# A chunked state-space scan on one core: the triangular solve taken for two units together, and three operand loads moved in the queue

## The reference, cut to what matters

```python
def step(s, inp):
    q_, w_, k_, v_, a_, b_ = inp
    sa = jnp.einsum('bhij,bhj->bhi', s, a_)
    s = s * w_[:, :, None, :] + sa[..., None] * b_[:, :, None, :] + v_[..., None] * k_[:, :, None, :]
    return (s, jnp.einsum('bhij,bhj->bhi', s, q_))
_, y = jax.lax.scan(step, s0, (qt, wt, kt, vt, at, bt))
```

## Time and profile before

| | |
|---|---|
| median of 3 runs | 6624.89 us (6621.29 to 6627.57) |
| the profiled execution | 6620.48 us |
| its span, first to last instruction | 6618.7 us |
| the scan | about 1435 to 2910 us of it |
| busy in 1700 to 2700 us | PE 879, weight loads 862, DVE 892, POOL 729, ACT 489 us |
| DMA engines there | busy 0.60, 131 GB/s, nearly all on SP's queue |
| granted TensorE clock there | 1.00 (2.4 GHz) |
| solve steps (L1167, L1171) | 960 + 960, 330.2 + 326.6 us on DVE |
| b and k expansions (L954) | 1024, 419.3 us on POOL |

### The profile page before, as it was taken

How to read it: one execution, slowest core, us unless ns; L and a number is a source line. 1 busy time by engine, 2 the same in 40 slices (tenths; PEclk the granted TensorE clock), 3 DMA queues, 4 the chain that set the end, 5 groups by cost and what they waited for, 6 DMA issues and landing times. The chain is left out here.

```text
span 6618.7 us, 201409 instructions
## 1 busy us (share of the span) xinstructions
PE 5523.2 (83%) x70816; PEld 4552.2 (69%) x70816; DVE 4142.5 (63%) x13289; ACT 3445.6 (52%) x10441; POOL 2667.4 (40%) x3872
## 2 busy tenths in 40 slices
PE   5555556648888888866599999999979999999999
PEld 4555555548888888854477777777757777777777
DVE  4666666658888989944355555555535555555555
ACT  3555555534444444434355555555535555555555
POOL 1333332236777777720133333333324343333433
PEclk7777777779999999986799999999989999999999
DMA  2222223335565566545200000000010000000000
GB/s 60 62 62 58 61 62 64 64 84 131 129 133 129 130 133 131 130 104 182 93 15 12 14 12 15 12 14 12 15 40 16 19 17 17 20 17 19 17 17 17
DMA packets 999524, 387.22 MB, mean 59 GB/s; under 512 B 775664, under 2 KB 948720, under 8 KB 998512
## 3 DMA queue, kind: packets, MB, share of 16 engines
q1 hardware_dynamic: 998192, 384.78, 24.7%
q10 hardware_dynamic: 1088, 0.00, 0.0%
HBM read 216.32 MB, written 168.30 MB: 58 GB/s over the span
## 5 line engine op out<-in xcount | busy, mean ns | idle before, releaser
L1584 POOL TENSOR_TENSOR l_pn<-l_prob,l_rinv 128x512 f32<-128x512 f32 x512 | 532.2, 1039 | 1430.5 <-DVE l_rinv L1684 1430.1
L1882 ACT ACTIVATE l_prob<-l_prob,l_nb,l_rq 128x256 f32<-128x256 f32 x1024 | 605.0, 592 | 436.7 <-DVE l_nb L1704 359.1
L437 POOL TENSOR_TENSOR cprev<-cum,sg 128x256 f32<-128x256 f32 x64 | 60.4, 962 | 784.2 <-DVE cum L355 784.2
L1171 DVE TENSOR_TENSOR sc_sol<-sc_sol,sc_step 128x15 f32<-128x15 f32 (+7 forms) x960 | 326.6, 340 | 33.0
L1167 DVE TENSOR_TENSOR sc_step<-sc_prob,sc_sol 128x15 f32<-128x15 f32 (+7 forms) x960 | 330.2, 344 | 26.6
L933 POOL TENSOR_TENSOR sc_ax<-sc_late,sc_headmask 128x256 f32<-128x256 f32 x256 | 173.1, 676 | 398.0 <-DMA sc_tok<-scratch_tok 361.0
L1597 POOL TENSOR_TENSOR l_outt<-l_t,l_xat 128x256 f32<-128x256 f32 x64 | 46.4, 726 | 624.8 <-DVE l_t L1766 624.8
L1062 ACT ACTIVATE sc_d_qk<-sc_part,sc_headmask 128x64 f32<-128x64 f32 x1024 | 270.2, 336 | 43.8 <-DMA sc_part<-scratch_part 43.8
L992 PE MATMUL sc_AB<-sc_early,sc_bx 64*64 64x64 f32 x4096 | 176.0, 223 | 125.8 <-POOL sc_kx L933 107.8
L1062 ACT ACTIVATE sc_d_qb<-sc_part,sc_headmask 128x64 f32<-128x64 f32 x1024 | 271.7, 339 | 0.0
L992 PEld LDWEIGHTS sc_AB<-sc_early,sc_bx 64*64 64x64 f32 x4096 | 152.9, 139 | 132.0 <-issue 131.9
(11 more groups left out here) (383 smaller groups left out, 19049.2 us busy)
## 6 DMA issues: line engine op xcount, KB each, us to landing
scratch_cm<-cm SPq DMA_DIRECT2D x64, 512.0 KB, 4.2
sc_early<-scratch_cm SPq DMA_DIRECT2D x128, 256.0 KB, 3.3
scratch_part<-sc_att SPq DMA_DIRECT2D x64, 512.0 KB, 4.3
sc_part<-scratch_part SPq DMA_DIRECT2D x64, 512.0 KB, 5.2
scratch_tok<-vt SPq DMA_DIRECT2D x512, 48.0 KB, 1.8
l_h<-scratch_h SPq DMA_DIRECT2D x128, 129.0 KB, 2.6
scratch_gr<-gr SPq DMA_DIRECT2D x64, 256.0 KB, 4.1
sc_late<-scratch_cm SPq DMA_DIRECT2D x64, 256.0 KB, 3.9
```

The lines of the kernel that those rows point to most:

```text
L437: nc.gpsimd.tensor_tensor(cprev[b][:], cum[b][:], sg[b][:], ALU.subtract).then_inc(S["cprev"][b].sem, 1)
L1171: ins = nc.vector.tensor_tensor(x[:, 0:rows, m + 1:CH], x[:, 0:rows, m + 1:CH], prod, ALU.add)
L1584: tt(pn[s][:, pair], prob[s][:, pair], rinv[s][:, pair].unsqueeze(2).broadcast_to([P, 2, 2 * P]), ALU.mult).then_inc(Q["pn"][s].sem, 1)
L1882: last_ = nc.scalar.activation(prob[s][:, h], prob[s][:, h], ACT.Exp, scale=rq8[s][:, h:h + 1], bias=nb[s][:, h:h + 1], accum_out=sums[s][ ...
```

## The change

Three things change in the scan.

1. `solve` takes both units of a window together: `sc_prob` and `sc_sol` hold two matrices in each partition, each step's instructions have twice the elements, and there are half as many. The steps stand in chunks 1, 2 and 3 of the even unit and in chunk 0 of the odd one, for the next window (`steps`). The problem of the next window is loaded at the start of the even unit, when both halves have been stored; the solution is stored near the start of the odd unit. The first window is solved before the loop, after the masking of unit (1, 0).
2. `load_late` stands in the middle of a unit and for the unit two ahead; `load_t` for the odd unit stands at the even unit's start, for the even unit in the odd one's middle.
3. The b and k tokens come by two DMAs into two tiles, and `expand` spreads each with one instruction of 256 columns instead of two of 128.

```diff
@@ -729,7 +729,7 @@
         sb = lambda n, s: ctx.enter_context(nc.sbuf_tensor("sc_" + n, s, F32))
         early = [sb(f"early{j}", [P, 2, 2, NB, CC, 2, CH]) for j in range(UC // 2)]
         late = [sb(f"late{k}", [P, UC, NB, CC, 2, CH]) for k in range(2)]
-        tok = [sb(f"tok{k}", [P, UC, NB, 2, CC, HS]) for k in range(2)]
+        tokb, tokk = ([sb(f"{n}{k}", [P, UC, BG, HS]) for k in range(2)] for n in ("tokb", "tokk"))
...
@@ -738,9 +738,8 @@
         part = [sb(f"part{k}", [P, UC, BG, 4, CH]) for k in range(2)]
         tt = [sb(f"tt{k}", [P, UC, BG, CH]) for k in range(2)]
         d_ak, d_t, d_qb, d_qk = ([sb(f"{n}{k}", [P, BG, HQ, CH]) for k in range(2)] for n in ("d_ak", "d_t", "d_qb", "d_qk"))
-        prob = [sb(f"prob{k}", [P, CH, CH]) for k in range(2)]
-        sol = [sb(f"sol{k}", [P, CH, CH]) for k in range(2)]
-        step_ = sb("step", [P, CH * CH])
+        prob, sol = sb("prob", [P, 2, CH, CH]), sb("sol", [P, 2, CH, CH])
+        step_ = sb("step", [P, 2 * (CH // 2) * (CH // 2)])
...
@@ -759,10 +758,10 @@
 
         pair = signals(nc, ctx, "early_in:16 v_in:16", UC // 2, "sl")
 
-        Hf = signals(nc, ctx, "late_in:32 gl_in:16 part_in:16 tt_in:16 att_out:16 part_out:16 prob_in:16 solved inv_out:16 "
+        Hf = signals(nc, ctx, "late_in:48 gl_in:16 part_in:16 tt_in:16 att_out:16 part_out:16 "
                      "sum mean dev ysq var lnv rs yn", 2, "sh")
-        Wn = signals(nc, ctx, "y_out:128", 1, "sw")
-        y_out = Wn["y_out"][0]
+        Wn = signals(nc, ctx, "y_out:128 prob_in:16 solved inv_out:16", 1, "sw")
+        y_out, prob_in, solved, inv_out = (Wn[n][0] for n in ("y_out", "prob_in", "solved", "inv_out"))
...
@@ -823,9 +822,10 @@
                     sp.dma_start(late[k][:].rearrange("p c b g y t -> p c (b g y t)"),
                                  a["cm"][bass.ds(w, 1), :, k * UC:(k + 1) * UC, 0].rearrange("o p c b g y t -> (o p) c (b g y t)")
                                  ).then_inc(Hf["late_in"][k].sem, 16)
-                    sp.dma_start(tok[k][:].rearrange("p c b x g i -> p (c b) (x g i)"),
-                                 a["tok"][bass.ds(w, 1), :, k * UC:(k + 1) * UC, :, 1:3].rearrange("o p c b x g i -> (o p) (c b) (x g i)")
-                                 ).then_inc(Hf["late_in"][k].sem, 16)
+                    for x, dst in ((1, tokb), (2, tokk)):
+                        sp.dma_start(dst[k][:].rearrange("p c (b g) i -> p (c b) (g i)", b=NB),
+                                     a["tok"][bass.ds(w, 1), :, k * UC:(k + 1) * UC, :, x].rearrange("o p c b g i -> (o p) (c b) (g i)")
+                                     ).then_inc(Hf["late_in"][k].sem, 16)
 
...
@@ -850,20 +850,24 @@
                     sp.dma_start(a["part"][u].rearrange("o p n -> (o p) n"), att[k][:].rearrange("p c q z t -> p (c q z t)")
                                  ).then_inc(Hf["part_out"][k].sem, 16)
 
-                def load_problem(w, k):
-                    sp.wait_ge(Hf["att_out"][k].sem, Hf["att_out"][k].after(w))
-                    sp.wait_ge(Hf["solved"][k].sem, Hf["solved"][k].after(w, 1))
-                    sp.dma_start(prob[k][:], a["att"][bass.ds(w * 2 + k, 1)].rearrange("o q h m t -> (o q h) m t")
-                                 ).then_inc(Hf["prob_in"][k].sem, 16)
-
-                def store_solution(w, k):
-                    sp.wait_ge(Hf["solved"][k].sem, Hf["solved"][k].after(w))
-                    sp.dma_start(a["inv"][bass.ds(w * 2 + k, 1)].rearrange("o q h m t -> (o q h) m t"), sol[k][:]
-                                 ).then_inc(Hf["inv_out"][k].sem, 16)
+                def load_problem(w):
+                    for k in range(2):
+                        sp.wait_ge(Hf["att_out"][k].sem, Hf["att_out"][k].after(w))
+                    sp.wait_ge(solved.sem, solved.after(w, 1))
+                    sp.sem_inc(s_free, 1)
+                    sp.dma_start(prob[:].rearrange("p o m t -> p o (m t)"),
+                                 a["att"][bass.ds(w * 2, 2)].rearrange("o q h m t -> (q h) o (m t)")).then_inc(prob_in.sem, 16)
+
+                def store_solution(w):
+                    sp.wait_ge(solved.sem, solved.after(w))
+                    sp.sem_inc(s_free, 1)
+                    sp.dma_start(a["inv"][bass.ds(w * 2, 2)].rearrange("o q h m t -> (q h) o (m t)"),
+                                 sol[:].rearrange("p o m t -> p o (m t)")).then_inc(inv_out.sem, 16)
 
                 def load_t(w, k):
-                    sp.wait_ge(Hf["inv_out"][k].sem, Hf["inv_out"][k].after(w))
+                    sp.wait_ge(inv_out.sem, inv_out.after(w))
                     freed("d_t", first_chunk(w, k) - 1 - UC)
+                    sp.sem_inc(s_free, 1)
                     sp.dma_start(tt[k][:], a["inv"][bass.ds(w * 2 + k, 1)].rearrange("o (c q) h m t -> (o h m) c q t", c=UC)
                                  ).then_inc(Hf["tt_in"][k].sem, 16)
 
@@ -878,46 +882,50 @@
...
                 def unit(w, k):
                     heads = (range(HP // 2, HP) if k else range(HP // 2)) if not isinstance(w, int) or w > 0 else range(0)
                     if exists(w, k, 1):
-                        n1 = shift(w, k, 1)
-                        load_late(*n1)
-                        load_part(*n1)
-                        load_t(*n1)
-                        load_gl(*n1)
-                    if exists(w, k, 3):
-                        load_problem(*shift(w, k, 3))
+                        load_part(*shift(w, k, 1))
+                        load_gl(*shift(w, k, 1))
+                    if not k:
+                        load_t(w, 1)
+                        if exists(w, k, 3):
+                            load_problem(w + 1)
                     if k and len(heads):
                         store_y(w - 1, heads)
-                    for j in range(UC // 2):
-                        if exists(w, k, LEAD + 1):
-                            load_early(*shift(w, k, LEAD + 1), j)
-                        if exists(w, k, 1):
-                            load_v(*shift(w, k, 1), j)
+                    if k and exists(w, k, 1):
+                        store_solution(w + 1)
+                    if exists(w, k, LEAD + 1):
+                        load_early(*shift(w, k, LEAD + 1), 0)
+                    if exists(w, k, 1):
+                        load_v(*shift(w, k, 1), 0)
                     if exists(w, k, 2):
-                        store_solution(*shift(w, k, 2))
+                        load_late(*shift(w, k, 2))
+                    if k and exists(w, k, 1):
+                        load_t(w + 1, 0)
+                    if exists(w, k, LEAD + 1):
+                        load_early(*shift(w, k, LEAD + 1), 1)
+                    if exists(w, k, 1):
+                        load_v(*shift(w, k, 1), 1)
                     if exists(w, k, LEAD):
                         pose(*shift(w, k, LEAD))
                     if not k and len(heads):
@@ -949,12 +957,8 @@
                     pool.wait_ge(S["y_ps"].sem, S["y_ps"].after(n, UC))
                     expand(ax[c], bg(late[k][:, c, :, :, 0, :]))
                     expand(qx[c], bg(late[k][:, c, :, :, 1, :])).then_inc(S["ax_x"].sem, 1)
-                    for dst, x in ((bT, 0), (kT, 1)):
-                        for b in range(NB):
-                            last = nc.gpsimd.tensor_tensor(
-                                dst[c][:, b * CC:(b + 1) * CC], tok[k][:, c, b, x].unsqueeze(2).broadcast_to([P, CC, HQ, HS]),
-                                headmask[:].unsqueeze(1).unsqueeze(3).broadcast_to([P, CC, HQ, HS]), ALU.mult)
-                    last.then_inc(S["kT_x"].sem, 1)
+                    expand(bT[c], tokb[k][:, c])
+                    expand(kT[c], tokk[k][:, c]).then_inc(S["kT_x"].sem, 1)
 
                 pool.wait_ge(s_c, 48)
...
@@ -1152,28 +1156,29 @@
                     diagonal(d_ak[c % 2], part[k][:, c, :, 2, :], S["d_ak"])
                     diagonal(d_t[c % 2], tt[k][:, c], S["d_t"])
 
-                def solve(w, k, m0, m1):
-
-                    x = sol[k]
+                def solve(w, m0, m1):
+
+                    x = sol
                     if m0 == 0:
-                        dve.wait_ge(Hf["prob_in"][k].sem, Hf["prob_in"][k].after(w))
-                        dve.wait_ge(Hf["inv_out"][k].sem, Hf["inv_out"][k].after(w, 1))
-                        nc.vector.tensor_copy(x[:], eye[:]).then_inc(s_chain, 1)
+                        dve.wait_ge(prob_in.sem, prob_in.after(w))
+                        dve.wait_ge(inv_out.sem, inv_out.after(w, 1))
+                        nc.vector.tensor_copy(x[:], eye[:].unsqueeze(1).broadcast_to([P, 2, CH, CH])).then_inc(s_chain, 1)
                         chain[0] += 1
                     for m in range(m0, m1):
                         rows, cols = m + 1, CH - 1 - m
-                        prod = step_[:, 0:rows * cols].rearrange("p (r t) -> p r t", r=rows)
+                        both = [P, 2, rows, cols]
```

(15 more changed lines are left out.)

27 lines of the change are left out of this document (12 added, 15 removed).

## The result

The changed kernel takes 6732.16 us (median of 4 runs, 6727.94 to 6736.50), the kernel before beside it 6626.23 us (6621.29 to 6634.49): ratio 1.0159, 95% interval 1.0141 to 1.0176. It is 106 us slower, and the forecast had been 6583. The profiled execution has a span of 6732.7 us, 114 more than before.

A forecast was written before the change was run, and what follows sets the result against it. PE's floor of 37.3 us a pair plus 7.1 lost to POOL's token wait and late DVE work bound the scan. Pairs from 44.36 to 43.3 save 33, the start 9: median 6583 us, range 6553 to 6601.

The forecast's parts named there:

- a2: Chunk 2 of a pair's even unit: DVE late, POOL done early, so solve steps run alone; 4.6 us.
- b0: Chunk 0 of a pair's odd unit: masking, statistics, expansions and six short solve steps; 4.6 us.
- a1: Chunk 1 of the even unit: problem wait 2.0 us, then eight solve steps; ends 13.8 us after T0.
- a3: Chunk 3 of the even unit: masking, expansions and eight solve steps, partly beside POOL; 6.3 us.
- T0: Zero of a pair's time count in us: the state instruction that ends b3.
- b3: Chunk 3 of the odd unit: no solve steps, PE's pace of 4.66 us; doubt whether the solution lands in time.
- The start: Start of the scan: first solve moved behind masking, one solve for two units; 9 us gained, bounds 3 and 14.
- 1 and 2: Rivals without a wait for the problem, the second with fewer DVE-POOL meetings: 6518 us (chance 0.25) and 6459 (0.06).
- 3: Rival: transfer burst not shortened, problem at T0 + 11.6 to 12, pair 44.5 us, kernel 6620; chance 0.10.
- 4: Rival: DMA burst stretched, problem lands after T0 + 12.7, pair 46.4 us at T0 + 14, kernel 6679; chance 0.10.
- 5: Rival: POOL instructions also wait out DVE's solve steps, pair 46.9 us, kernel 6695; chance 0.03.
- closing signs of being wrong: Prediction wrong if PE is bound by something unlisted, such as a late odd-unit solution, or the pair exceeds 44.4 us.

The follow-up runs named there:

- warm4: Changed kernel with extra PE matmuls into an unused bank, 24 ahead of chunk 2 and 16 ahead of chunk 0 of every unit; 6725.89 us, ratio 1.0134.
- narrow: Changed kernel with b and k expanded by four 128-wide POOL instructions a chunk, split transfers kept; 6702.88 us, ratio 1.0122.
- early_problem: Changed kernel with the problem's load put ahead of all other loads of the even unit; 6687.03 us, ratio 1.0080.
- no_solve: Changed kernel without 14 of the solve's 15 steps, loads and stores kept; 6503.44 us, ratio 0.9803.
- late_mid: Kernel before with only late operands and tokens moved to a unit's middle, for the unit two ahead; 6576.62 us, ratio 0.9913.
- lead6_narrow: Changed kernel with products six units ahead, paired solve spread over seven chunks, loads earlier, and narrow b and k expansions; 6466.71 us, ratio 0.9745.
- lead6: Changed kernel with products six units ahead, paired solve spread over seven chunks, problem and solutions loaded earlier; 6477.97 us, ratio 0.9784.

## Why the prediction was wrong

*The step that failed* is the sum's "a2: ... DVE is alone: 4.6" and "b0: ... 4.6". It took the pace of undelayed passes for chunks that begin right behind an idle PE, where the same sum had given a1 4.5 us over PE's pace. The first passes there run at 1.2 GHz, 1.31 and 1.56 us are lost, and warm4 gives just these back. With them at 6.2 the sum would have been 46.5, and the forecast slower than before. For b0 a second term is needed: with a3 at its forecast 6.3 the idle time ahead of b0 would have been some 1.5 us (an estimate, 2.29 less 0.76), and narrow lost nothing in b0 behind 1.57.

*Mis-sized terms.* a1 was 9.54 for 9.14, and right only by luck, because two errors met: DVE asked at T0 + 8.6 and not 7.0, since I had reckoned with the short variance reduction (0.4) where the mean and the deviation stand (2213.97 to 2215.57, 1.6), and so waited 1.1 and not 2.0. The work without the wait is 8.35 (early_problem), not 7.1. a3 was 7.06 for 6.3: `sc_yn` (0.6) stands in it and was left out. Together 0.4 + 0.76. b3's 0.41 is the late solution that the prediction named as its last doubt; it lands late in a part of the pairs only, but narrow (b3 6.74) and no_solve (7.30) show that it takes back much of a gain elsewhere. 0.27 in a0 and 0.14 in b1 I have not followed up.

*What held.* POOL's wait for tokens went, and late_mid shows this part to be a gain by itself. Steps beside POOL cost 0.57 each in a1 (0.62 for the widest, in a3) and quiet ones 0.24 to 0.33. Narrow expansions are the better ones (narrow, lead6_narrow), by 0.4% each. This agrees with what the prediction took from the page "SBUF — State Buffer" of the Trainium skill (section "Who interferes with whom") and held against the wide ones.

*What held by luck.* The problem landed at T0 + 9.7 (8.3 to 9.7), but not on the path forecast. SP was held 1.82 us and not 4.38, so the problem was issued at 2213.98, T0 + 5.5, 4.4 us after its store, where the forecast's numbers make T0 + 6.7 to 7.6. Then it took 4.2 us to land, and not 1.7 to 2.2.

*The start.* Nine microseconds were forecast. The first state update comes 3.5 us earlier (1490.51 instead of 1494.0) and the sum that stands just before the second one 5.5 us earlier (1497.55 instead of 1503.04). The solve begins later than before, behind the masking of four more chunks (copy at 1462.22 for 1456.11), and takes 15.3 us (to 1477.56) where the forecast had about 10, since most of its steps meet POOL; and the first chunk still waits for the solution's trip through HBM.

*The rivals.* 1 and 2 were no: there is a wait, and early_problem, which takes it away, is still at 1.0080. 3 had the landing time wrong. 4, the forecast's side-changer, had the right sign with the wrong mechanism: the problem was not later than forecast. 5 is out: POOL's instructions stay 0.57 apart in a1. The true mechanism stood in no rival, and the 0.13 for slower had been summed over a late transfer and a lock between DVE and POOL alone. Both of the prediction's closing signs of being wrong came true: the odd unit's solution was late for b3, and the pair was above 44.4.

*Where 48.47 - 44.36 = 4.1 a pair comes from.* Over PE's pace the pair lost 7.1 us before and loses 11.2 now. The late operands' move by itself gave 1.6 (late_mid). Against it stand the solve's 30 instructions gathered in four chunks: a1 is 4.9 over PE's 4.66 (1.1 of it the wait for the problem) and a3 2.4, a2 and b0 are 3.1 over it (2.8 the clock), and b3 loses 0.4 to the solution load, while b1 and b2, which had carried steps too, are at PE's pace or 0.15 over it. Halving the number of the solve's instructions (DVE's busy time 892 to 671 us in 1000) bought nothing, because DVE's work was no longer spread where PE could hide it. lead6 with the same instructions, spread, and its loads earlier, is some 250 us faster than the changed kernel.
